# Linear attention: the denominators as 32-column matmuls in four column groups, their inverses spread over the partitions through memory

## What is computed

```python
q = elu(x @ Wq) + 1; k = elu(x @ Wk) + 1; v = x @ Wv        # 16 heads of 64
a = sigmoid(x @ Wa + ba + 2)                               # one decay per token and head
# scan over the tokens of a sequence
S = a_t * S + k_t v_t^T ;  z = a_t * z + k_t
out_t = (q_t S) / (q_t z + 1e-6)
y = out @ Wo ;  x1 = layernorm(x + y)
```

## Time and profile before

| | |
|---|---|
| median of 3 runs | 1423.08 us (1421.81 to 1424.44) |
| the profiled execution, its own time | 1418.74 us |
| its span, first to last instruction | 1416.9 us |
| mean granted TensorE clock | 0.958 of full speed |
| PE busy | 1279.9 us (90%) |
| DVE, ACT, POOL busy | 832.9 (59%), 952.1 (67%), 734.5 us (52%) |
| linear attention | from the start to about 715 us |
| DMA | 151.30 MB, mean 107 GB/s |

### The profile page before, as it was taken

The page is one execution under the profiler, slowest core; times in us unless marked ns, Lnnn a source line. Parts: engine busy times, 40 slices in busy tenths (PEclk is TensorE's granted clock), DMA queues, the critical chain, the costliest instruction groups (busy, mean ns, idle before and its releaser), DMA issues. The chain is left out here.

```text
span 1416.9 us, 30100 instructions
## 1 busy us (share of the span) xinstructions
PE 1279.9 (90%) x10053; PEld 1077.0 (76%) x10053; DVE 832.9 (59%) x1643; ACT 952.1 (67%) x2120; POOL 734.5 (52%) x835
## 2 busy tenths in 40 slices
PE   5899999999999999999889999953599999998780
PEld 4788888888888888888767777743488888888780
DVE  4344555544555545555468888847366666666564
ACT  4677777777777777777747777754465666655453
POOL 0244444444444444444648777720467777776653
PEclk9999999999999999999999999975699999999895
DMA  4333222122222222222133433323356666666737
GB/s 153 94 102 85 86 80 79 62 81 78 84 76 76 61 84 75 84 70 75 61 117 83 117 104 97 95 76 96 115 130 157 157 164 157 158 161 152 183 62 244
DMA packets 155791, 151.30 MB, mean 107 GB/s; under 512 B 48882, under 2 KB 124250, under 8 KB 155674
## 3 DMA queue, kind: packets, MB, share of 16 engines
q1 hardware_dynamic: 140698, 129.18, 30.1%
q0 software_dynamic: 14976, 20.62, 8.1%
HBM read 113.45 MB, written 33.84 MB: 104 GB/s over the span
## 5 line engine op out<-in xcount | busy, mean ns | idle before, releaser
L362 POOL TENSOR_SCALAR_AFFINE_SELECT a_decay<-a_decay 128x256 f32<-128x256 f32 x256 | 110.2, 434 | 250.2 <-ACT a_decay L440 250.2
L561 DVE TENSOR_TENSOR a_probs<-a_ps_s,a_decay 128x384 f32<-128x384 f32 x256 | 135.0, 554 | 160.4 <-PE a_ps_o L725 121.5
L371 POOL TENSOR_TENSOR a_key_sum<-a_probs 128x256 f32<-128x256 f32 x128 | 97.3, 760 | 158.0 <-DVE a_probs L561 158.0
L1843 POOL DMA_INDIRECT sum_rows<-e_y_out,e_target x78 | 126.1, 1617 | 80.4 <-ACT e_y_out L1897 56.6
L413 ACT ACTIVATE a_qk_exp<-a_ps_qk 128x512 f32<-128x512 f32 x128 | 76.6, 599 | 130.8 <-PE a_ps_qk L656 124.0
L554 DVE SCALAR_TENSOR_TENSOR a_qk<-a_qk_exp,a_qk_relu 128x512 f32<-128x512 f32 x128 | 90.1, 704 | 114.7 <-ACT a_qk_relu L414 114.5
L656 PE MATMUL a_ps_qk<-a_xT_hi,a_w_hi 128*128 128x256 f32 x512 | 144.7, 283 | 4.9 <-ACT a_qk_relu L414 3.9
L656 PE MATMUL a_ps_qk<-a_xT_lo,a_w_hi 128*128 128x256 f32 x512 | 143.6, 280 | 0.0
L656 PE MATMUL a_ps_qk<-a_xT_hi,a_w_lo 128*128 128x256 f32 x512 | 143.6, 280 | 0.0
L438 ACT ACTIVATE a_decay<-a_c_rows,a_c_col 128x256 f32<-128x256 f32 x256 | 129.6, 506 | 0.0
L1824 POOL DMA_INDIRECT e_x_in<-x_rows,e_index x78 | 80.3, 1030 | 80.2 <-DVE e_index L1989 57.7
(11 more groups left out here) (297 smaller groups left out, 3871.6 us busy)
## 6 DMA issues: line engine op xcount, KB each, us to landing
a_c_rows<-a_c_scratch SPq DMA_DIRECT2D x128, 256.0 KB, 3.1
e_gu_raw<-in_L_ffn_gate_w SPq DMA_DIRECT2D x23, 512.0 KB
e_gu_raw<-in_L_ffn_up_w SPq DMA_DIRECT2D x23, 512.0 KB
e_dn_raw<-in_L_ffn_down_w SPq DMA_DIRECT2D x23, 512.0 KB, 5.5
a_x_in<-in_x SPq DMA_DIRECT2D x16, 256.0 KB, 2.7
a_x_res<-in_x SPq DMA_DIRECT2D x16, 256.0 KB
x_rows<-a_x SPq DMA_DIRECT2D x16, 256.0 KB, 3.3
x_bo_rows<-a_x_bo SPq DMA_DIRECT2D x16, 256.0 KB, 3.9
```

What stands on the lines that cost most here:

```text
L362: pool.affine_select(out=d, in_=d, compare_op=ALU.is_ge, fill=0.0, base=0, pattern=[[0, 2], [1, P]], channel_multiplier=-1)\
L371: pool.tensor_tensor(key_sum[:], probs[:, :, P:N], probs[:, :, N:TRI], ALU.add).then_inc(keys_summed, 1)
L561: vec.tensor_tensor(probs[:, h, :], ps_s[h][:, 0:TRI], decay[h][:], ALU.mult)\
L1843: pool.indirect_dma_start(sum_dram, bass.IndirectOffsetOnAxis(target[par][:, blk:blk + 1], 0), y_out[par][:, blk, :], None, compute_op=ALU ...
```

## The change

The ones matrix gets 32 columns (`DENS`) in place of 64. The four denominators of a pair (two heads, two halves of the queries) go to four groups of 32 partitions, all on the same 128 columns of `ps_o`, with an explicit tile position for each; all four now come behind the wait for `key_sum`. ACT's two activations work on 128 x 128. What they give, `rden_row`, holds head 0's first half on partitions 0 to 31, its second on 32 to 63, and so on; SP writes one partition of each group to memory (4 x 128 numbers, `store_den`), waits for that, and reads them back, 256 numbers to 64 partitions for each head (`spread_den`, two DMAs). `normalise` waits for these.

The order changes too. On ACT `invert_den` now comes before `high_oT`; on DVE `normalise` comes behind `weigh`; on SP `spread_c` runs four slots ahead and sits between the store and the wait for it.

```diff
-        ones, scan_ones = sb("a_ones", [P, DH]), sb("a_scan_ones", [H, N])
+        ones, scan_ones = sb("a_ones", [P, DENS]), sb("a_scan_ones", [H, N])
...
+            def store_den(n):
+
+                sp.wait_ge(rden_done, n + 1)
+                sp.dma_start(rden_dram[n % 4], rden_row[n % 2][0:P:DENS, :]).then_inc(rden_stored, 16)
+
+            def spread_den(n):
+
+                sp.wait_ge(rden_stored, 16 * (n + 1))
+                if n >= 2:
+                    sp.wait_ge(oT_done, n - 1)
+                for h in range(2):
+                    row = rden_dram[n % 4, 2 * h:2 * h + 2, :].rearrange("(a t) i -> a (t i)", a=1)
+                    sp.dma_start(rden[n % 2][h * DH:(h + 1) * DH, :], row.to_broadcast([DH, N])).then_inc(rden_spread[n % 2], 16)
...
+                    n = b * PAIRS + g
+                    store_den(n)
+                    if g == 4 and b + 1 < B:
+                        store_c(b + 1)
+                    if g == 5 and b + 1 < B:
+                        spread_c(n + ROWS_AHEAD - 1)
+                    if g != 4 and n + ROWS_AHEAD < B * PAIRS:
+                        spread_c(n + ROWS_AHEAD)
+                    spread_den(n)
...
-                act.activation(ln_den[:], ps_o[g % 2][:, 1, :], ACT.Ln, bias=den_eps[:]).then_inc(ln_done, 1)
+                act.wait_ge(rden_done, n)
+                act.activation(ln_den[:], ps_o[g % 2][:, 1, 0:P], ACT.Ln, bias=den_eps[:]).then_inc(ln_done, 1)
                 act.wait_ge(ln_done, n + 1)
                 if exists(b, g, 2):
-                    act.wait_ge(oT_done, n - 1)
-                act.activation(rden[g % 2][:], ln_den[:], ACT.Exp, scale=-1.0).then_inc(rden_done, 1)
+                    act.wait_ge(rden_stored, 16 * (n - 1))
+                act.activation(rden_row[g % 2][:], ln_den[:], ACT.Exp, scale=-1.0).then_inc(rden_done, 1)
...
-                vec.wait_ge(rden_done, n + 1)
+                vec.wait_ge(rden_spread[g % 2], 32 * (n // 2 + 1))
...
-                for h in range(2):
-                    pe.matmul(out[h][:, 1, 0:P], ones[:], probs[:, h, 0:P], start=True, stop=True)
+                dens = [ps_o[g % 2][t * DENS:(t + 1) * DENS, 1, 0:P] for t in range(4)]
                 pe.wait_ge(keys_summed, n + 1)
                 for h in range(2):
-                    mm = pe.matmul(out[h][:, 1, P:N], ones[:], key_sum[:, h, :], start=True, stop=True)
+                    pe.matmul(dens[2 * h], ones[:], probs[:, h, 0:P], start=True, stop=True, tile_position=(0, 2 * h * DENS))
+                    mm = pe.matmul(dens[2 * h + 1], ones[:], key_sum[:, h, :], start=True, stop=True,
+                                   tile_position=(0, (2 * h + 1) * DENS))
```

40 lines of the change are left out of this document (18 added, 22 removed).

## The result

The changed kernel takes 1437.28 us (median of 4 runs, 1436.01 to 1439.57); the kernel before took 1422.44 on the same chip (1421.44 to 1424.44). The ratio is 1.0104, 95% interval [1.0086, 1.0122]. The forecast was 1417.7 with a range of 1406 to 1429: the time lies outside it, on the other side of no change. What happened is the rival "the memory trip decides", priced at 1440 and given a chance of 0.15.

The account below looks back on a forecast made before the run. PE was taken to bound the kernel through the linear attention, down to the last sequence. -10.8 + 1.0 + 1.2 + 3.2 = -5.4 us, from 1423.1 to 1417.7; range 1406 to 1429.

Parts of the forecast that it names:

- the memory trip decides: Rival: normalise two slots on waits for the store and reads; slower from about 5.25 us, 1440 at 5.7; chance 0.15.
- PE's part: Denominator matmuls: 0.22 us removed, 0.13 added for changing to 32-column groups; net 0.09 a pair, 10.8 over 120 slots.
- company in the queue: Trips of pair 5 and the first three sequences, sharing the queue with other reads: 1 us added in all.
- last sequence: Slots without projections, 3.43 us before, become some 3.6 because of the trip: 7 x 0.17 = 1.2 us more.
- the end: The last pair's trip stands bare: high_oT 3.9 us later, of which 0.7 is free; 3.2 us more.
- four groups do not run as side by side as two: Rival: two denominator steps take 0.29 us for 0.22, PE gains only 2.4 us; +3, 1426; chance 0.14.
- The two tie: Ordinary slots: the loop of ACT and DVE takes 4.28 us, the same as PE's new slot; cost nothing.
- The trip, "4.2": Store and read-back of the inverse on SP: 4.2 us, from 3.2 to 5.0, hidden in ordinary slots, which allow 4.74.
- The cushion up to 5.1: Before exp_qk: a lateness of some 0.55 us costs nothing, so PE loses only for trips from about 5.1 us on.

Follow-up runs that it names:

- e1: The changed kernel without the trip through memory, normalise taking the inverse straight from rden_row: 1407.94 us, 0.9908 of the kernel before.
- e13: The kernel before with only its 64-column ones matrix moved behind the stage's other tiles, a 32-column spacer in its place: 1419.46 us, ratio 0.9979.
- e6: The changed kernel with the x1 stores of the last but one sequence moved behind the last pair's reads: 1442.76 us, 1.0132 of the kernel before.
- e2: The kernel before with only the change's new order on ACT and DVE, 64-column denominators, no trip: 1425.11 us, ratio 1.0025.
- e10: The changed kernel with the second of two reads of c issued behind pair 5's reads: 1438.96 us, 1.0097 of the kernel before.

## Why the prediction was wrong, step by step

Forecast and measured difference, term by term (us, from the two profiles):

| term | forecast | measured |
|---|---|---|
| PE's part, 15 sequences | -10.8 | -14.0 (e1 against before) |
| company in the queue, 15 sequences | +1.0 | +17.4 (after against e1) |
| last sequence | +1.2 | +4.2 |
| the end | +3.2 | +8.4 |
| up to the first score; the rest | 0 | +1.5; -0.2 |
| sum | -5.4 | +17.3 |

**PE's part** was right: 0.09 us a pair forecast, 10.8 in all; e1's 15 sequences are 14.0 shorter than before's, and 10.0 shorter than e13's, whose operands lie as in the change. Its pieces: the denominators up to `add_y` went from 0.54 to 0.36 where I expected 0.32, the values from 0.70 to 0.80 where I expected 0.83. The change of shape to 32 columns costs 0.10 (I took 0.13 between 0 and 0.20), and the four groups start 7 ns after each other, which makes a step 0.134 for 0.11. Net 0.08 a pair, 9.6 in all. The rule of the Trainium skill that changing the tiling mode drains the array (TensorEngine Tiling (Array Packing), Key Properties) is borne out by the 0.10, and its figure for packing (TensorE: Matmul & The Clock Gate, Packing small matmuls), 3.07 for four row tiles, from which I had made an estimate of 0.29 for two steps, by 0.27 with four column tiles: the rival "four groups do not run as side by side as two" was half true, at 0.04 a pair.

The other 4.4 us were in no step of the forecast, and e13 shows what they are: the 32-column ones matrix makes room, and the operands of the projections, moved by it, are multiplied at 0.1135 us a step instead of 0.1145 to 0.1176. Why one place is better than the other stays open; no other place was tried.

**"The two tie"**: ACT and DVE's loop against PE's 4.28. Right. e1 holds 4.27 with PE always busy, and ACT's wait before `exp_qk` fell to almost nothing, as the text said.

**The trip, "4.2"**: mis-sized, and the first step that failed. A trip by itself takes 4.72 to 4.8: the store to the reads' issue 1.59 where I took 1.48, the read 2.65 where I took 2.4, and 0.50 for the issue of the second read, ahead of which I counted only the first's 0.33. The ends of my range for a trip alone, 3.2 and 5.0, held; the middle did not. The cushion up to 5.1 was close: trips of pair 5 of 5.14 to 5.23 us (sequences 7 to 9 and 13) leave the next slot 0 at 4.95, those of 5.25 to 5.29 cost it 0.14 to 0.21, one of 5.80 costs 0.79 and one of 6.41 1.48. So in this trace the limit lies near 5.2.

**"For pair 5 ... and for the first three sequences ... I add 1 us in all"**: this is the step that decided. Company in the queue cost 17.4 us over the 15 sequences (636.3 against e1's 618.9), of which 7.8 in slot 5 of sequences 0 to 2 (9.17, 6.22, 5.88 for 4.49) and 7.1 in slot 0 of sequences 1 to 7. Pair 5's trip is 5.14 to 6.41 in sequences 3 to 14, always beyond 5.1. Of the other pairs' trips 29 of 84 are, but a late trip does not cost the same everywhere: 17 of these are of pairs 7, 0 and 1, whose `normalise` falls in slots 1 to 3, in or just behind the long slots, and they stretch no slot of these sequences; pair 7's go up to 6.17. I had the rows for it, a landing of 3.0 at worst for a 16 KB store and 3.1 for the 256 KB reads beside it, and wrote them down as a rival. But I priced the sum with the medians, although one late trip of eight is enough to stop PE once a sequence. A trip with the landing of 3.0 in it was over 6 by my own text (by its middle terms 5.8).

**The last sequence, "1.2"**: 4.2. At 3.6 a slot there was no cushion, so the 0.55 by which the trip was priced too low enters in full: two slots hold one trip, 7 x 0.55 / 2 = 1.9 more. The rest, 1.1, goes with late trips: pair 7 of sequence 14 took 5.51 and pair 4 of the last sequence 5.60, and `normalise` waited 0.90 and 1.37 for them.

**The end, "3.2"**: 8.4. The trip's own 5.36 behind the logarithm became 8.78 (724.42 - 715.64 up to `high_oT`). Of this 2.8 is the company of the x1 stores issued at 716.09 and 716.72, just ahead of the last store, which I had overlooked; e6, with these stores behind the reads, gets 1.9 of it back. 0.55 is the trip's own. Another 1.3 is there without a trip (e1: 16.4 for 15.1) and comes with the new order (e2: 16.7). 3.2 + 2.8 + 0.55 + 1.3 = 7.9, and 0.5 stays unexplained.

**The start** was not in the forecast at all: 1.5 us. It is not the change's: e10, the same up to there, reaches the first score at 42.8. It is told below.

**The chances.** The rival's mechanism and place were right and its threshold close. That its price came out (1440, measured 1437.3) is in part luck: it took a trip of 5.7 in every slot, where the median was 4.88 outside pair 5 and single late trips did the harm; 7.8 of the 17.4 come from the next stage's loads, which it did not count; and the end cost 8.4 for its 4.7. Its 0.15 was too little: its three conditions (a queue with 256 KB a slot in it, a limit 0.5 us above the priced trip, a loop that one late trip stops) all stood in the rows.

## What to carry to other kernels

A round trip through memory that must be over within a fixed number of slots is priced by its slow cases in the queue that it really shares, not by the median landing: count every issue in it, look at what else the queue moves in that slot, and ask how many late ones of a period it takes to stop the bound engine. A gain of 0.1 us on the bound engine can be taken with a few short copies on an engine that has room, but slot by slot: only where that engine is idle at that moment, and with the old form kept where it is not and in the drain at the end.
